# Matmuls with unread results placed in four waits of TensorE, in the second layer of a four-layer cross-attention kernel

## The reference

```
xa  = ln(x, ln1_w, ln1_b)                  # the first norm
sx  = shift(xa)                            # previous row minus this row
xxx = tanh((xa + sx * maa_x) @ maa_w1)     # "hidden"
xm  = xa + sx * (maa_stack + xxx @ maa_w2) # five mixes: k, w, v, r, g
w, r, k, v, g = projections of the five mixes
out = scan over 256 steps, per head of 16  # s = k*v + w*s
og  = groupnorm(out) * gn_w + gn_b
x1  = x + og * g @ Wo.T
xc  = ln(x1, ln2_w, ln2_b)                 # the second norm
sx2 = shift(xc)
rr  = sigmoid((xc + sx2 * ffn_maa_r) @ Wfr.T)
kk  = square(relu((xc + sx2 * ffn_maa_k) @ Wfk.T))
out = x1 + rr * (kk @ Wfv.T)
```

## Time and profile before

| | us |
|---|---|
| median of 3 runs | 4183.42 |
| lowest and highest | 4180.28, 4185.7 |
| the profiled execution's own time | 4177.29 |
| its span | 4175.8 |
| TensorE busy in the span | 3928.9 (94%) |
| VectorE busy | 2936.9 (70%) |
| ScalarE busy | 1925.1 (46%) |
| GpSimd busy | 1600.2 (38%) |
| mean granted TensorE clock, share of full speed | 0.979 |

### The profile page before, as it was taken

How to read it: one execution, slowest core, us unless ns; L and a number is a source line. 1 busy time by engine, 2 the same in 40 slices (tenths; PEclk the granted TensorE clock), 3 DMA queues, 4 the chain that set the end, 5 groups by cost and what they waited for, 6 DMA issues and landing times. The chain is left out here.

```text
span 4175.8 us, 68031 instructions
## 1 busy us (share of the span) xinstructions
PE 3928.9 (94%) x20588; PEld 2965.3 (71%) x20588; DVE 2936.9 (70%) x6438; ACT 1925.1 (46%) x3836; POOL 1600.2 (38%) x1100
## 2 busy tenths in 40 slices
PE   7999995789999987999999999999999999999989
PEld 3333334567777755888977988877888877978866
DVE  6767653788888874767767758757767757767653
ACT  4666662223333323555543555534555534555522
POOL 1443432566666641332244332344232344333230
PEclk8999997999999998999999999999999999999999
DMA  5444423000000002222223222223121122122122
GB/s 165 131 122 138 127 67 128 11 6 16 16 16 16 11 11 85 71 66 78 67 66 107 62 77 66 66 74 105 57 92 59 60 79 90 61 92 73 52 78 99
DMA packets 158840, 298.56 MB, mean 71 GB/s; under 512 B 18628, under 2 KB 41540, under 8 KB 157392
## 3 DMA queue, kind: packets, MB, share of 16 engines
q1 hardware_dynamic: 156568, 291.06, 22.3%
q0 software_dynamic: 1008, 3.67, 0.2%
q10 hardware_dynamic: 1032, 0.97, 0.1%
HBM read 254.21 MB, written 42.21 MB: 71 GB/s over the span
## 5 line engine op out<-in xcount | busy, mean ns | idle before, releaser
L2209 POOL TENSOR_TENSOR c_wl<-c_wr,c_wh 128x512 fp32r<-128x512 f32 (+1 forms) x576 | 822.1, 1439 | 1600.5 <-ACT c_wh L2589 1362.5
L2690 ACT ACTIVATE c_pr<-c_ps,c_nms 128x257 f32<-128x257 f32 x512 | 244.2, 477 | 472.9 <-DVE c_nms L2929 471.0
L1738 DVE TENSOR_TENSOR_SCAN b_sb<-b_wt,b_s,b_ps 128x256 f32<-128x256 f32 x512 | 361.0, 736 | 16.1 <-PE b_ps L1189 4.2
L843 DVE TENSOR_REDUCE a_nm<-a_ps 128x2 f32<-128x1024 f32 x256 | 312.0, 1223 | 71.5 <-PE a_ps L490 70.8
L2589 ACT ACTIVATE c_wh<-c_wr 128x512 fp32r<-128x512 f32 (+1 forms) x464 | 315.4, 688 | 44.5 <-PE c_ps L2296 40.7
L1673 POOL TENSOR_TENSOR b_sb<-b_sb,b_rt 128x1024 f32<-128x1024 f32 x128 | 277.8, 2177 | 145.7 <-DVE b_sb L1738 95.8
L686 ACT ACTIVATE a_ex<-a_ps 128x1024 f32<-128x1024 f32 x256 | 260.6, 1022 | 150.0 <-PE a_ps L510 148.0
L2294 PE MATMUL c_ps<-c_hh,c_wh 128*128 128x512 f32 x768 | 307.6, 400 | 7.3 <-DVE c_hl L2795 7.3
L2294 PE MATMUL c_ps<-c_gh,c_wh 128*128 128x512 f32 x768 | 307.6, 401 | 5.3 <-DVE c_gl L2972 2.7
L2296 PE MATMUL c_ps<-c_hh,c_wl 128*128 128x512 f32 x768 | 304.5, 396 | 0.0
L2295 PE MATMUL c_ps<-c_hl,c_wh 128*128 128x512 f32 x768 | 304.0, 396 | 0.0
(11 more groups left out here) (378 smaller groups left out, 9939.6 us busy)
## 6 DMA issues: line engine op xcount, KB each, us to landing
c_wr<-in_downs SPq DMA_DIRECT2D x192, 256.0 KB, 2.6
c_wr<-in_wv SPq DMA_DIRECT2D x64, 512.0 KB, 3.8
c_wr<-in_wk SPq DMA_DIRECT2D x128, 256.0 KB, 2.9
c_wr<-in_wq SPq DMA_DIRECT2D x128, 256.0 KB, 2.6
a_qp<-strips SPq DMA_DIRECT2D x64, 256.0 KB, 4.4
a_kp<-strips SPq DMA_DIRECT2D x64, 256.0 KB, 4.5
c_wr<-in_fc SPq DMA_DIRECT2D x64, 256.0 KB, 2.8
strips<-a_qh SPq DMA_DIRECT2D x32, 256.0 KB
```

Of the source, the lines that this page charges most:

```text
L843: dve.tensor_reduce(NM[:, s, :].rearrange("p (h c) -> p h c", h=HG)[:, 2 * p:2 * p + 2, c:c + 1], ps[:, bank:bank + 2, :], AX.X, ALU.max, ...
L1738: mm = dve.tensor_tensor_scan(SB[:, quad % RING, pr % 2, e, 1:L + 1], WT[:, third(b, i), e, :], half(spread_bank(pair), e), S0[:, b, 2 * i ...
L2209: pool.tensor_tensor(piece(WL, slot), piece(WR, slot), piece(WH, slot), ALU.subtract).then_inc(piece_cut[slot], 1)
L2690: act.activation(PR[:, i, 0:L + 1], ps[:, BS + 1 - i % 2, 0:L + 1], ACT.Exp, bias=NMS[:, i:i + 1], scale=float(K2) ** -0.5, accum_out=RS[: ...
```

## The change

A helper `keep_busy(count)` issues `count` fp32 matmuls of the constant tile with itself into the first 128 columns of PSUM bank `PA`; they carry no semaphore and nothing reads their result. It is called with 8 before the first batch's wait for its load, with 16 between the first batch's `mean` and `var`, with 64 behind the first batch's `var`, and with 58 behind the last batch's second `var`. Nothing else differs.

```diff
+        WARM = (8, 16, 64, 58)
...
+            def keep_busy(count):
+                for _ in range(count):
+                    pe.matmul(ps[:, PA, 0:P], MEANW[:, :], MEANW[:, :], start=True, stop=True, skip_group_check=True)
+
...
                 t = due(slot, PE_AT["mean"])
                 if t is not None:
+                    if t == 0:
+                        keep_busy(WARM[0])
                     pe.wait_ge(x_in, (t + 1) * 16 + AHEAD)
...
                     mm.then_inc(a_mean, 1)
+                    if t == 0:
+                        keep_busy(WARM[1])
                 t = due(slot, PE_AT["var"])
                 if t is not None:
...
                     mm.then_inc(a_var, 1)
+                    if t == 0:
+                        keep_busy(WARM[2])
                 t = due(slot, PE_AT["hidden"])
...
                 mm.then_inc(p_var, 1)
+                keep_busy(WARM[3])
                 pe.wait_ge(fk_in, s + 1 + AHEAD)
                 pe.wait_ge(p_sd, s + 1 + AHEAD)
```

## The result

The changed kernel takes 4190.87 us (median of 11 runs, 4186.57 to 4195.14) against 4180.28 for the kernel before in its 11 runs: ratio 1.0025, 95% interval 1.0016 to 1.0034, so 7 to 14 us slower, 10.6 by the medians. The forecast was 3.4 us slower. A second set of 11 runs of the same kernel gave 1.0021 (1.0012 to 1.0030). The profiled execution took 4189.71 us, its span is 4188.2.

A forecast was written before the change was run, and what follows sets the result against it. The prediction took layer 1 as a TensorE-bound pipeline with a loose start. Net +2.3 us at hidden and +1.1 us at the last batch gave +3.4, added to the median 4183.42: 4186.8 us, range 4178 to 4194.

The forecast's parts named there:

- The direction: Whole kernel: slower by 3.4 us, since the filler is longer than three of the waits.
- the unit: Cost of one filler record: 0.111 us at full clock (0.222 us per program matmul), 0.213 us at half clock.
- The first rival (the filler fits): All calls: at 0.06 us per record they delay nothing and the clock stays up, -6.8 us, 4176.6 us; chance 0.10.
- the unraised clock: All calls: the constant tile does not raise or hold the clock, 27 to 39 us slower, about 4216 us; chance 0.04.
- the late instructions: Third call: an instruction fetch queues behind weight loads and stretches the filler by 8.8 us, 4195.6 us; chance 0.10.
- the rule that the prediction weighed: Skill's N / 2.4 + 2.5 ns, 56 ns for 128 columns; per program matmul, third call 3.6 us, fourth 3.2, nothing late.
- Second, third and fourth call: Second: var takes 1.99 us in place of 3.78; third: net +2.3 us at hidden's end; fourth: net +1.1 us.
- First call: Layer 1's start, before mean: 3.4 us of filler, mostly inside the load wait; mean ends 0.4 us sooner.
- The sum: Whole kernel: +2.3 at hidden and +1.1 at the last batch give +3.4 us, with 6.2 us of lost clock won back.
- The rival of the absorbed delay: Start of layer 1: something other than hidden ends the start-up, so only the last call counts, +1.1 us, 4184.5; chance 0.08.
- the cold stretches "can fall otherwise": Layer 1, 700 to 900 us: lower-clock stretches may shift between runs; a reason given for the range 4181 to 4192 us.
- the forecast's own range: Whole kernel: 4181 to 4192 us, with chance 0.68 for the forecast; the runs of before spread over 5.4 us.

The follow-up runs named there:

- sizes that fit: Changed kernel with call sizes 0, 11, 40, 40 in place of 8, 16, 64, 58: ratio 0.9991 against the kernel before, median 4176.33 us.
- increments on ScalarE and a first call of 4: Changed kernel with sizes 4, 11, 40, 40 and ScalarE issuing TensorE's third of the layer-start semaphore increments: ratio 0.9987 against the kernel before, median 4173.89 us.
- The run with the increments on ScalarE: Changed kernel, sizes kept, with ScalarE issuing TensorE's third of the layer-start semaphore increments: ratio 1.0017 against the kernel before, median 4187.96 us.
- changed kernel again: The changed kernel run once more, unchanged: ratio 1.0021 against the kernel before, median 4189.88 us.

## Why the prediction was right or wrong

**The direction, and the unit, were right.** 128 records took 14.45 us, (14.45 - 0.275) / 127 = 0.112 us each. Of the 16 at half clock (3.75 us) the second starts 0.34 us after the first and the last takes 0.42 us, so that the others start (3.75 - 0.34 - 0.42) / 14 = 0.213 us apart. Both are the forecast values: the tile's constant content changes nothing, and line 3136 was the row to go by. The first rival (the filler fits), the unraised clock and the late instructions fall with it: no gap is seen in any filler. As to the rule that the prediction weighed: the Trainium skill, page "TensorE: Matmul & The Clock Gate", section "Back-to-back issue gap", gives 56 ns as the gap of an isolated matmul and about 81 ns for 128 columns in a stream of weight loads and matmuls. The records of this case, 112 ns apart, agree with neither.

**Second, third and fourth call: right.** From the end of mean to the end of var 1.0 us was gained, as forecast; from there to the end of hidden 3.7 us were lost (forecast: 5.1 of overrun, 1.4 back); at the end 3.75 us late and 2.61 back, +1.1. The run with sizes that fit turned the sign of just these terms.

**First call: wrong, and this is the failed step.** "TensorE is let go when GpSimd's last memset ends" made the call start at 652.5, 2.5 us ahead of the load, so that only 0.9 us of its 3.4 would show and the earlier clock would pay for that. It starts 2.35 us after the memset, when the load (3.2 us to landing before, 3.4 after, counted from its issue) has just landed too, and delays mean by its whole length; mean ends 2.7 us late where -0.4 was forecast (1.5 and 2.6 us late in the second and third profile, in which the clock rose 3.4 and 5.6 us after the first filler record and not 5.9). In the rows of before, mean's wait was put down to the load, and the prediction took the 654.99 at which mean starts for the landing. The load landed at 654.47, 3.24 us after its issue; the increments ended about 0.4 us behind it, and one row cannot show the second of two that end so close together. So the load did not even set the start of mean in the kernel before: in all six profiles without a first call mean starts 2.49 to 2.51 us after the last memset, though the load landed anywhere from 1.95 to 2.08 us after it, and with the increments on ScalarE and a first call of 4 it starts after 2.04. "issue" as the releaser of the first weight load, not quoted there, was the hint. The run with the increments on ScalarE shows it.

**The sum.** With +2.7 for the first call the rows give +5.3 at hidden and +1.1 at the end, 6.5 us. By the means of three profiles of each the start costs 31.67 - 26.62 = 5.1 us and the end 34.04 - 32.81 = 1.2, together 6.3. Measured were 10.6 and 8.7 us, with intervals that reach down to 6.7 and 5.0. The 2.0 us between the mean middles (891.4 and 889.4) bring 6.3 to 8.3; with three profiles each and two lengths 5 us apart that can be chance, and is not shown to be the change's.

It may not be chance alone. If the start and the end (against the means 26.62 and 32.81 of the kernel before) are reckoned in the same way for all eight sets of runs without fillers in the middle, the measured difference of the medians lies above the rows every time: by 2.4 to 4.3 us in the five sets whose kernel has the calls of 16 and 64 in its start, by 1.0 to 1.5 us in the other three. No run says where these microseconds are, so between 2 and 4 of the 10.6 us stay unexplained.

That 4190.87 lies inside the stated 4178 to 4194 is partly luck. The forecast of 4186.8 stands on the median of three runs, 4183.42, and the 11 runs have 4180.28, 3.1 us lower. This hides 3.1 of the 7.2 us by which the effect of the change was forecast too small (3.4 against 10.6), a factor of three.

**The rival of the absorbed delay fell,** since what hidden lost was found again at the start of the last batch in every profile, apart from the two lengths of the middle. That the cold stretches "can fall otherwise" was right, but I had their size too small: 5.4 us between the middles of two executions of one kernel, more than the forecast effect, and the forecast's own range was built on the spread of 3 runs.

## What to carry to other kernels

Matmuls whose result nobody reads do hold TensorE's clock up, but they stand in its queue like any other: size them from a row of the same form so that they end before the operand they wait for, here 40 and not 64 or 58 (4 us won, with an interval that just reaches none, in place of 10 lost). Before filling the wait at a block's start, find out when the engine itself is free; semaphore instructions are not in the trace, and a wait that says "load" can hide a second one that ends with it. A clock that rises pays only where TensorE is on the chain: filling the first batch's waits as well took another 5 us off (ratio 0.9974 in place of 0.9987; with the second batch's it is 0.9973, 4167.07 us, the fastest kernel here). The rows show only part of this: the middle is 886.2 and 886.4 us in these two profiles, 1 to 2 us under the short length of the others and 6 to 7 under the long one. Filling the second batch's waits took nothing off. VectorE is busy 80 of the 92 us there; that it bounds the stretch is argued from this and not shown. Two profiles pass it in 90.6 and 90.7 us (changed kernel again; fitting sizes with a first call of 4), with three instructions of VectorE fewer in it, 118 in place of 121.

## What the runs showed of the hardware that was not expected

The same kernel has a middle of 887 to 888 us or of 893 us from one execution to the next, and with it goes the time that the middle spends at the lower clock: 58 to 61 us against 72 us over twelve profiles of eight kernels. Where the clock rises after TensorE has taken up work differs too, even for the same kernel: 5.9, 3.4 and 5.6 us after the first filler record in the three profiles of the changed kernel, 3.0 and 5.1 us at two places of the kernel before. In the second profile of the kernel before it rose at 658.6 us, behind `mean` alone, and `var` took 1.99 us without any filler, so that part of what a filler buys can come by itself. In every profile in which TensorE did its own third of the increments its first matmul of the layer came 2.3 to 2.5 us after the last memset, and 0.05 us after it where ScalarE did them.
